# Triple sums of a compressed interaction network: 64x32 TensorE tiles with listed products, in place of 128-partition lists of single fields

## What is computed

```python
h1 = einsum('bid,bjd,ijh->bhd', x, x, W0)
h2 = einsum('bid,bjd,ijh->bhd', x, h1, W1)
out = concatenate([h1, h2], axis=1).sum(axis=-1)      # 512 x 256
```

## Time and profile before

| | |
|---|---|
| median of 3 runs | 349.72 us |
| the profiled execution | 350.17 us |
| its span, first to last instruction | 348.3 us |
| busy: TensorE, its weight loads | 329.0 us, 292.8 us |
| busy: VectorE, ScalarE, GpSimd | 171.4 us, 114.7 us, 10.1 us |
| sums over partitions (L511), weighing (L545) | 126.2 us, 128.7 us busy |

### The profile page before, as it was taken

How to read it: one execution, slowest core, us unless ns; L and a number is a source line. 1 busy time by engine, 2 the same in 40 slices (tenths; PEclk the granted TensorE clock), 3 DMA queues, 4 the chain that set the end, 5 groups by cost and what they waited for, 6 DMA issues and landing times.

```text
span 348.3 us, 11398 instructions
## 1 busy us (share of the span) xinstructions
PE 329.0 (94%) x5397; PEld 292.8 (84%) x5397; DVE 171.4 (49%) x212; ACT 114.7 (33%) x210; POOL 10.1 (3%) x14
## 2 busy tenths in 40 slices
PE   0899997999889999999999999999999999999997
PEld 0566664555779999998999999899999999999996
DVE  2205469467899385444536572635358090812000
ACT  1366653343542243060306214230522332142300
POOL 9200000000000000000000000000000000000000
PEclk9999999899999999999999999999999999999999
DMA  7950431300040003700000090000006000000000
GB/s 301 385 117 2 155 146 32 122 1 0 2 154 4 2 2 77 229 4 2 19 2 2 13 274 25 0 19 2 4 3 154 2 2 17 4 2 4 4 0 15
DMA packets 4350, 20.03 MB, mean 58 GB/s; under 512 B 592, under 2 KB 1104, under 8 KB 3920
## 3 DMA queue, kind: packets, MB, share of 16 engines
q1 hardware_dynamic: 3728, 18.79, 16.8%
q10 hardware_dynamic: 576, 0.52, 0.5%
HBM read 18.78 MB, written 0.52 MB: 55 GB/s over the span
## 4 chain that ended last, share of the span: by engine, by line
PE 90%; DVE 6%; DMA 1%; ACT 1%; issue 0%; SPq 0%; DVEq 0%
PE out_ps L545 37%; PE stage L511 32%; PE stage L473 8%; PE stage L487 7%; PE stage L493 4%; PE stage L476 2%; DVE arena L354 2%; DMA arena<-in_w_rows 1%; DVE arena L287 1%; DVE arena L400 1%; DVE arena L362 1%; DVE arena L359 1%; DVE arena L375 0%; ACT arena L423 0%; DVE arena L323 0%
## 5 line engine op out<-in xcount | busy, mean ns | idle before, releaser
L545 PE MATMUL out_ps<-arena 114*128 114x128 f32 (+2 forms) x968 | 128.7, 294 | 0.5 <-ACT arena L440 0.5
L511 PE MATMUL stage<-arena 128*60 128x80 f32 (+4 forms) x4096 | 126.2, 227 | 3.1 <-DVE arena L354 2.1
L511 PEld LDWEIGHTS stage<-arena 128*50 128x50 f32 (+2 forms) x4096 | 123.8, 128 | 5.3 <-issue 3.3
L545 PEld LDWEIGHTS out_ps<-arena 114*128 114x128 f32 (+1 forms) x968 | 121.7, 192 | 5.8 <-ACT arena L440 0.6
L440 ACT COPY arena<-stage 114x480 f32<-114x480 f32 (+4 forms) x136 | 72.5, 540 | 138.9 <-PE stage L511 138.9
L354 DVE TENSOR_TENSOR arena<-arena 128x3200 f32<-128x3200 f32 x16 | 55.7, 3486 | 28.4 <-PE stage L511 28.3
L473 PE MATMUL stage<-arena 128*128 128x380 f32 (+1 forms) x78 | 34.3, 523 | 10.1 <-DVE arena L289 10.1
L487 PE MATMUL stage<-arena 128*114 128x512 f32 (+1 forms) x60 | 31.5, 608 | 3.1 <-DVE arena L375 3.1
L357 DVE TENSOR_TENSOR arena<-arena 128x640 f32<-128x640 f32 x16 | 13.2, 824 | 39.2 <-PE stage L511 39.2
L362 DVE TENSOR_TENSOR arena<-arena 128x800 f32<-128x800 f32 x32 | 30.2, 985 | 0.0
L414 ACT COPY arena<-stage 128x480 f32<-128x480 f32 (+1 forms) x39 | 22.1, 568 | 22.5 <-PE stage L476 22.5
(11 more groups left out here) (22 smaller groups left out, 43.5 us busy)
## 6 DMA issues: line engine op xcount, KB each, us to landing
arena<-in_x_dense SPq DMA_DIRECT2D x8, 640.0 KB, 7.0
arena<-in_x_single SPq DMA_DIRECT2D x16, 320.0 KB, 5.0
arena<-in_c_first SPq DMA_DIRECT2D x1, 2560.0 KB, 9.1
arena<-in_w SPq DMA_DIRECT2D x2, 640.0 KB, 7.0
arena<-in_c_second SPq DMA_DIRECT2D x1, 1280.0 KB, 6.4
arena<-in_w SPq DMA_DIRECT2D x1, 1216.0 KB, 9.8
arena<-in_w_square SPq DMA_DIRECT2D x1, 800.0 KB, 4.3
arena<-in_c_one SPq DMA_DIRECT2D x2, 256.0 KB, 10.1
```

Of the source, the lines that this page charges most:

```text
L511: done = nc.tensor.matmul(bank[PART * part:PART * part + r1 - r0, 0:count * 2 * some] .rearrange("p (i b) -> p b i", b=2 * some)[:, 2 * (t ...
L545: done = nc.tensor.matmul(to, sums, w, start=tile == 0 and s == 0, stop=last, skip_group_check=True)
```

## The change

Setup multiplies `W1` of each field with a list of all 780 unordered pairs of `W0`, in two banks of 390 columns. VectorE and GpSimd assemble from `y` the weights of 105 slots of 128 rows in `z`, in many small pieces; one stage of 105 transposes turns them. The matmul L487 and the adds L375 are gone.

In the main part the roles turn round. The stationary operand is now a window of 32 single fields of one batch row (64 partitions x 32 columns), the moving operand a list of 49 to 115 products. Eight such 64x32 tiles fit the array: 2 on the partitions (`s`, one of the two rows) by 4 columns. A pair of rows takes 12 matmuls, 460 moving columns for each `s`, and fills one slot row of 128 partitions x 115. VectorE makes the 420 products of a pair (8 pairs a "unit", 20 instructions); GpSimd copies the single fields beside them (4 copies a unit, 10 columns of 8 pairs each). `PRODS = 2` units. The weighing is 115 matmuls of 128 columns a batch, 14 or 15 after each unit of the next batch, and all 115 of the last batch at the end. The core of the diff:

```diff
-    PROD = HALF_PAIRS * W_ROWS
-    PRODS = 3
+    PROD = 4 * LISTED
+    PRODS, WS, DS = 2, 3, 3
...
+        Y_PARTS = [(0, Y_WIDTH // 2), (Y_WIDTH // 2, Y_WIDTH)]
+        TURNS = [(k, min(FOUR, PAIRED - k)) for k in range(0, PAIRED, FOUR)]
...
@@ GpSimd @@
+            pool.wait_ge(emptied, Y_BANKS_A)
+            within_blocks("PQS")
+            shared_by_two(("PQ", "QS", "SP"))
+            pool.wait_ge(emptied, Y_BANKS)
+            within_blocks("pqs")
...
+            shared_by_two(("pq", "qs", "sp")).then_inc(z_copied, 1)
+            for u in range(UNITS):
+                pool.wait_ge(w_loaded[u % WS], 16 * (u // WS + 1))
+                if u < PRODS:
+                    pool.wait_ge(z_ready, 1)
+                else:
+                    pool.wait_ge(filled, filled_through_unit(u - PRODS))
+                for column in range(4):
+                    done = nc.gpsimd.tensor_copy(
+                        view(prod0 + u % PRODS * UNIT * PROD + column * LISTED, (PROD, UNIT), (1, SINGLES)),
+                        view(w_0 + u % WS * UNIT * W_WORDS + SINGLES_AT[column], (W_WORDS, UNIT), (1, SINGLES)))
+                done.then_inc(singles_ready, 1)
@@ VectorE @@
+            dve.wait_ge(emptied, Y_BANKS_A)
+            mixed_of_rectangles(("PQ", "QS", "SP"), own=False)
+            mixed_of_triangles("PQS", own=False)
+            dve.wait_ge(emptied, Y_BANKS)
+            mixed_of_triangles("pqs", own=False)
+            mixed_of_rectangles(("pq", "qs", "sp"), own=False).then_inc(z_begun, 1)
+            dve.wait_ge(z_begun, 1)
+            dve.wait_ge(z_copied, 1)
+            mixed_of_rectangles(("PQ", "QS", "SP", "pq", "qs", "sp"), own=True)
+            mixed_of_triangles("PQSpqs", own=True)
+            shared_terms().then_inc(z_ready, 1)
+            dve.wait_ge(z_ready, 1)
+            for u in range(UNITS):
+                products(u)
@@ TensorE @@
-                for part, (r0, r1) in enumerate([(0, FIRST_PART[tile]), (FIRST_PART[tile], rows)]):
-                    done = nc.tensor.matmul(
-                        bank[PART * part:PART * part + r1 - r0, 0:count * 2 * some]
-                        .rearrange("p (i b) -> p b i", b=2 * some)[:, 2 * (t - t0):2 * (t - t0) + 2, :],
-                        view(prod0[(2 * p + hf) % PRODS] + in_unit * W_ROWS + r0, (1, r1 - r0)),
-                        view(single0 + t * SLOTS + first, (PAIRS * SLOTS, 2), (1, count)), start=True, stop=True)
+            ORDER = [(0, 0), (3, 0), (0, 1), (3, 1), (1, 0), (2, 0)]
+                if half == 0:
+                    pe.wait_ge(w_loaded[u % WS], 16 * (u // WS + 1))
+                    pe.wait_ge(singles_ready, u + 1)
+                    pe.wait_ge(prod_ready, u + 1)
+                pe.wait_ge(emptied, emptied_through_four(q - 3) if q >= 3 else SETUP_BANKS)
+                for r in range(FOUR):
+                    t = half + r
+                    for column, part in ORDER:
+                        w, a, b = PARTS[column][part]
+                        for s in range(2):
+                            rows = (s * P // 2, (s + 1) * P // 2)
+                            done = nc.tensor.matmul(
+                                banks[2 * q % RING + s][WIDE * column:WIDE * (column + 1), 0:LISTED * FOUR]
+                                .rearrange("p (n b) -> p b n", b=FOUR)[:, r, a:b],
+                                view(w_0 + (u % WS * UNIT + t) * W_WORDS + WINDOW_AT[w], (1, WIDE), rows=rows),
+                                view(prod0 + (u % PRODS * UNIT + t) * PROD + column * LISTED + a, (1, b - a), rows=rows),
+                                start=True, stop=True)
...
+            for u in range(UNITS):
+                for q in range(u * UNIT // FOUR, (u + 1) * UNIT // FOUR):
+                    sum_four(q)
+                n, v = divmod(u, IN_BATCH)
+                if n >= 1:
+                    for k in range(v * LISTED // IN_BATCH, (v + 1) * LISTED // IN_BATCH):
+                        weigh(n - 1, k)
+            for k in range(LISTED):
+                weigh(BATCHES - 1, k)
```

More of the change, by code:

```diff
@@ L15 @@
 from contextlib import ExitStack
+from itertools import product as every
 import concourse.bass as bass
@@ L23 @@
 FIELDS = 39
[L24 to L49, removed]
@@ L52, in x_pairs @@
[L52 to L64, removed]
+BLOCKS = {"P": (0, 7), "Q": (7, 7), "S": (14, 7), "p": (21, 6), "q": (27, 6), "s": (33, 6), "A": (0, 20), "B": (21, 18)}
@@ new lines, with affine @@
+W0_PAIRS = w0_pairs()
+Y_WIDTH = len(W0_PAIRS)
+Y_COLUMN = {frozenset(pair): c for c, pair in enumerate(W0_PAIRS)}
+assert Y_WIDTH == FIELDS * (FIELDS + 1) // 2
+def affine(at, counts):
+    zero = (0,) * len(counts)
+    start = at(*zero)
+    steps = [at(*(zero[:k] + (1,) + zero[k + 1:])) - start if n > 1 else 0 for k, n in enumerate(counts)]
+    for index in every(*(range(n) for n in counts)):
+        assert at(*index) == start + sum(s * i for s, i in zip(steps, index))
+    return start, list(zip(steps, counts))
@@ L110, in cin_kernel @@
[L110 to L131, removed]
+        c0 = take(PAIRED * HID)
@@ L171, in in_fours @@
[L171 to L188, removed]
@@ L203, in banks_through @@
[L203 to L217, removed]
+        W1_PIECES = [(0, 6), (6, 18), (18, FIELDS)]
@@ new lines, in z_at, with triangle_runs @@
+        def z_at(column, w, slot, i):
+            return z0 + (slot - SINGLES) * B + WIDE * column + window(w).index(i)
+        def triangle_runs():
+            for column, slot, w, x in TRIANGLES:
+                fields = block(x)
+                for m in range(len(fields)):
+                    for part in WINDOWS[w]:
+                        yield column, slot + run_slot(len(fields), m), w, x, fields, m, part
+        NOT_MET = {("QS", 1, "Q"), ("QS", 2, "P"), ("SP", 2, "S"), ("sp", 3, "q"), ("pq", 3, "p"), ("pq", 4, "s")}
@@ new lines, in _ @@
+                for a, b in Y_PARTS:
+                    nc.tensor.matmul(claim(g)[:, 0:b - a], view(w1_0 + f * HID, (1, HID)), view(w0_0 + a, (1, b - a)),
+                                     start=True, stop=True).then_inc(filled, 1)
+                    g += 1
+            pe.wait_ge(ident_ready, 1)
+            pe.wait_ge(z_ready, 1)
+            for k, n in TURNS:
+                bank = claim(g)
+                for m in range(n):
+                    done = nc.tensor.transpose(bank[:, m * HID:(m + 1) * HID], view(z0 + (k + m) * B, (1, B)),
@@ L568 @@
     f32 = _np.float32
-    by_row = x.reshape(batch // 2, 2, fields, dim).transpose(1, 3, 0, 2).reshape(2 * dim, batch // 2, fields)
-    ones = _np.ones((2 * dim, batch // 2, 1), f32)
-    square = _np.zeros((hid, 40, 40), f32)
-    square[:, :fields, :fields] = w0.transpose(2, 0, 1)
-    rows, one = _np.zeros((2, hid, 2, W_SPAN + X_SPAN), f32), _np.zeros((2, 128, 4, hid), f32)
-    for half in range(2):
-        for r, (f, g) in enumerate(w_pairs(half) + x_pairs(half)):
-            if f == ONE or g == ONE:
-                continue
-            is_x = r >= W_ROWS
-            row = place(r - W_ROWS, X_FIRST) if is_x else place(r, W_FIRST)
-            tile, r = 2 * half + is_x, row + W_SPAN * is_x
-            rows[0, :, half, r] = one[0, row, tile] = w0[f, g]
-            if f != g:
-                rows[1, :, half, r] = one[1, row, tile] = w0[g, f]
@@ L594 @@
-    nc = _bacc.Bacc("TRN2", target_bir_lowering=False, num_devices=1)
+    by_row = x.reshape(batch // 128, 2, 64, fields, dim).transpose(1, 4, 0, 2, 3).reshape(2 * dim, batch // 2, fields)
+    lists = _np.zeros((2, hid, Y_WIDTH), f32)
+    for c, (f, g) in enumerate(W0_PAIRS):
+        lists[0, :, c] = w0[f, g]
+        if f != g:
+            lists[1, :, c] = w0[g, f]
+    c1, met = _np.zeros((2, 128, SINGLES, hid), f32), set()
+    for column in range(4):
+        w = PARTS[column][0][0]
+        for slot in range(SINGLES):
+            f = ROW_W[SINGLES_AT[column] + slot]
+            for row, i in enumerate(window(w)):
+                if frozenset((f, i)) not in met:
+                    met.add(frozenset((f, i)))
+                    c1[0, WIDE * column + row, slot] = w0[f, i]
+                    if f != i:
+                        c1[1, WIDE * column + row, slot] = w0[i, f]
```

563 lines of the change are left out of this document (253 added, 310 removed), and 3 rows, old and new, of the table RECTANGLES.

## The result

The changed kernel takes 360.9 us, the median of 4 runs (358.3 to 362.02), against 349.82 of the kernel before on the same chip: the ratio is 1.0305, 95% interval 1.024 to 1.0369. It is slower by 3%. The forecast was 329, faster. The profiled execution, the fastest of the four, took 358.3 us, its span 356.3.

What follows compares the result with a forecast made beforehand. VectorE was to become the bound: setup and start to 125.8 us, 30 units of 5.6 us (168) to 293.8, then last sums 1.9, weighing 3.4 and 25.7, end 2.5, and 1.87 around the span: 329.2 us, range 306 to 362.

Steps and rivals of the forecast that it cites:

- the bare end: After the last unit's sums: its weighing, 3.4 us, then the last batch's 115 weighing matmuls, 25.7 us, with nothing beside them.
- TensorE's unit of 5.25 us: Main part, 8 pairs with weighing: sums 1.84, weighing 3.21 and change of shape 0.2 us, below VectorE's 5.6.
- Sums 1.84 us a unit: TensorE's sums of 8 pairs in the main part, at 0.23 us a pair with the tiles running together.
- my upper 0.25: TensorE's sums: us a pair worked out if it looks only six records ahead, against 0.205 with all tiles side by side.
- TensorE cannot start records fast enough: Rival, 20%: record starts bound TensorE's sums; at 23.3 ns a record a unit takes 7.9 us, 387 us in all.
- GpSimd's hold on VectorE: Main part: GpSimd's four copies of single fields hold VectorE up by 0.77 us a unit, bounds 0 and 0.88.
- VectorE's own 4.85 us: Main part: VectorE's 20 instructions and 3360 elements a unit take 4.85 us, without any hold by GpSimd.
- ScalarE sets the pace of the transposes: Setup, 105 transposes: ScalarE's copies of 512 columns at 0.586 us, 26 of them, outlast four transposes at full clock, 0.44.
- the adds that read far apart: Setup, VectorE's bare adds making z: 43.9 us in all, 11 us less if far-apart elements cost no more than neighbours.
- the price of weighing: TensorE in the main part: 0.223 us a weighing matmul, plus 0.2 us for the change between sums and weighing.
- the clock: TensorE idle in setup: first transposes at half clock, 1.0 us more; first-batch sums at lower clock, 3.7 us, fit in 5.6.
- the forecast's estimate of 0.198 for a tile alone: TensorE's sums: a tile's 115 moving columns in one matmul take 198 ns a pair.

Runs made afterwards that it cites:

- The ninth kernel: Kernel before the change, all 16 passes cut to the shortest sums, only the last pass weighed: 3.73 us per 128 records, 7.5 us a pass between added pauses.
- the 8-matmul kernel: Whole changed kernel with 8 matmuls a pair instead of 12, same moving columns, part of the sums against the wrong window: 320.44 us, ratio 0.916.
- the finer weighing: Changed kernel with the weighing spread after every 4 pairs instead of every 8, nothing left out: 355.75 us, ratio 1.0159.
- three kernels with 256, 384 and 512 instructions a unit: Changed kernel's main part cut to TensorE's sums, with 8, 12 and 16 matmuls a pair: spans 264.0, 325.1 and 382.6 us.

## Why the prediction was wrong

The forecast against the profiled execution, in us:

| | forecast | measured |
|---|---|---|
| first matmul | 6.5 | 6.7 |
| products of W1 copied | 62.1 | 60.2 |
| z done, transposes begin | 106.0 | 100.4 |
| sums begin | 123.8 | 116.4 |
| last sums end | 295.7 | 324.5 |
| last weighing ends | 324.8 | 353.7 |

Setup was 7.4 us lighter than forecast, and the bare end, 3.4 + 25.7, came to 29.2. The error is all in "sums and weighing", 208.1 us instead of 171.9, where the step was: from 125.8 on, 30 units of 5.6 us, with VectorE as the bound. The first batch's eight units were to take 37.5 us of this and took 42.9; the other 24 were to take 134.4 and took 165.2. From the first weighing to the end of the sums the chain that ended last gives the pace (start us, us, records):

```profile
164.07 4.73 PE out_ps L513 x28
324.51 29.24 PE out_ps L513 x260
```

The 260 records are the weighing of the last unit (30) and of the last batch (230), so 23 units lie between the two starts: 6.98 us each.

**The step that failed** is TensorE's unit of 5.25 us, which counted only what TensorE does with its instructions and not how they come. Two terms of it were wrong:

- Sums 1.84 us a unit, measured 2.39 in one piece: 0.30 us a pair, not 0.23, nor my upper 0.25. With weighing and the change of shape, 3.32 or 3.54, that is 5.8 us and not 5.25.
- Nothing stood for the supply. A unit has 384 instructions of sums and 57 of weighing, 441, or 1.72 lots; at 3.64 us a lot that alone is 6.3. The next lot comes while TensorE weighs, but a lot full of sums is used up in 1.6 us, before the next can come; so work and supply add in part, to 6.98. The pauses are 1.2 us of it, or 27 us in 23 units. By this estimate the kernel would have taken some 331 us without them, so it is the missing term that turned a gain into a loss.

Of the rivals, "TensorE cannot start records fast enough" had the side and the point of decision right (slower from 6.44 us a unit on; it is 6.98), the mechanism and the price wrong. It was worked out from a start rate of 23.3 ns a record, and gave 387 us. Records start every 12.45 ns when they are there. The evidence for it, 23.8 ns in one pass, I had rightly explained by the width of the weights; what I did not ask was whether a stretch of 512 instructions, two lots, says anything about 14,000 in a row. The ninth kernel shows that it does not. The Trainium skill's "TensorEngine Tiling (Array Packing)", section "Instruction Overhead", gives some 60 cycles for each matmul. As a bound on starts across tiles this case refutes it: at 2.4 GHz that is 25 ns, and records start every 12.45.

**GpSimd's hold on VectorE**, 0.77 us a unit in the forecast, is 0.18. VectorE's own 4.85 us were 5.0. Neither set the pace of the changed kernel: VectorE waits for TensorE 49.9 us. The price of two engines reading at once falls on GpSimd. Where VectorE stands idle in the 8-matmul kernel, copies start 0.19 us apart (154.93, 155.12, 155.31), as the forecast took them; beside VectorE's multiplications it is 0.375. And in three units of the changed kernel the four copies took four times as long as the 1.5 us above, one of them 3.24 us:

```profile
141.93 5.84 POOL L265 COPY arena<-arena 128x80 f32<-128x80 f32 x4 [3.12 <-PE stage L493]
```

In the 8-matmul kernel, where VectorE has fewer gaps, single copies took up to 4.4 us, and TensorE had to wait for them. GpSimd's times in a profile are rough, but TensorE goes on when such a copy ends (one from 136.31 to 140.71, TensorE from 140.81). Its list of waits:

```profile
PE stage L493 <- POOL arena L265: 10.4, 5, 4.4
```

The Trainium skill, "SBUF — State Buffer", section "Who interferes with whom", has the ports that the two engines share as an exclusive lock, which a VectorE instruction with two inputs in SBUF and a GpSimd instruction that reads SBUF both need. That they hold each other up is seen here, but not shared out evenly: VectorE lost 0.18 us beside 1.5 us of copies, and a copy was held for longer than any one multiplication lasts (0.56 us in the mean for the largest).

**Right** were the stages of setup, that ScalarE sets the pace of the transposes (a copy every 0.48 us where 0.586 was taken, 16.1 us in all for 17.8), the adds that read far apart (40 us bare, forecast 43.9), the price of weighing (28 records in 3.32 us are 0.237 us a matmul with one change of shape), and the clock. In the wait for VectorE and at the first transposes it was at its lower level, and again in the first batch, where TensorE had pauses in every lot (columns: us, busy and records of each engine, clock, DMA):

```profile
100.36:102.50 2.14, 2.14 (x10) 2.14 (x11) 2.14 (x8) 0.75 (x2) 2.12 (x8) 0.50 0.01 4
129.40:146.50 17.10, 12.13 (x593) 10.15 (x579) 15.60 (x62) 6.63 (x14) 7.58 (x12) 0.50 0.36 108
```

That the first batch's sums run at 1.2 GHz costs little, as forecast, though for another reason than VectorE's pace: most of what they wait for is instructions. A lot took 3.5 to 4.1 us at the higher clock (121.08 to 129) and 3.5 to 3.9 in the next three at the lower. Three times in this batch they do wait for VectorE, 2.8 us in all.

**Where the gain went.** TensorE's busy time fell by 65 us, 38 of them in the sums (126.2 to 88.0) and 16 in the weighing (128.7 to 112.3). 40 us are given back in setup, where TensorE stands idle from 59.7 to 100.4, and 37 us in the pauses of the main part (33.0 + 4.4 in the list of waits). The 8-matmul kernel, which takes part of the sums against the wrong window but keeps all else, shows what the layout would be worth with a third fewer sum instructions: 8% under the kernel before. Of the versions that compute the reference none beats it; the best is the finer weighing, 1.6% above.

## What to carry to other kernels

Count instructions, not only columns: before splitting matmuls into small tiles, work out how many instructions a stretch of some ten microseconds needs on one engine, and set that against 256 in 3.6 us (14 ns each; a float32 matmul is four). A rate that a trace shows over one or two lots is not a rate that can be kept. In a profile the sign is an idle time "issue" in mid stream, at record counts that are multiples of 128, less the semaphore instructions among them; spreading slow instructions evenly among fast ones hides some of it but costs changes of shape (5 us won here where 12 were expected), fewer instructions hide nearly all of it.

## What the hardware showed that I had not expected

- TensorE's instructions come in lots of 256, and where TensorE uses them up faster, a new lot comes 3.56 to 3.64 us after the last in the mean whatever is in it (three kernels with 256, 384 and 512 instructions a unit), 3.73 in a fourth. Loads of the windows at the same time made no difference (325.1 and 325.2 us).
- Eight 64x32 tiles with different moving data do run together: 460 moving columns for each of two rows in 0.21 us with 8 matmuls, against the forecast's estimate of 0.198 for a tile alone. With 12 or 16 matmuls it is 0.28 to 0.30.
- A copy of 80 elements on GpSimd takes 0.19 us from start to start alone, 0.375 beside VectorE's two-input multiplications, and up to 4.4 us where VectorE runs without a gap.
- Runs of a kernel that waits for instructions scatter more, 358.3 to 362.02 us, than those of the kernel before, 349.63 to 350.23.
